# A convolution and selective-scan kernel: GpSimd multiplies two states at a time and takes over the sum of delta

## The reference

```python
xs = silu(conv5x5(x) + conv_b)                       # reshaped to (B, 96, 3136)
dts, Bs, Cs = split(einsum('kd,bdl->bkl', x_proj_w, xs))        # 6, 4, 4 rows
delta = softplus(einsum('dr,brl->bdl', dt_w, dts) + dt_b)
log_dA = maximum(delta[:, :, None, :] * A, LOG_EPS)  # A = -exp(A_logs), EPS = 1e-9
P = exp(cumsum(log_dA, axis=-1))
dB_u = delta[:, :, None, :] * Bs[:, None] * xs[:, :, None]
hs = P * cumsum(dB_u / maximum(P, EPS), axis=-1)
y = einsum('bdnl,bnl->bdl', hs, Cs) + xs * Ds
```

## Time and profile before

| | us |
|---|---|
| median of 3 runs | 4023.35 (4022.84 to 4023.77) |
| the profiled execution | 4020.36 |
| its span | 4018.6 |

### The profile page before, as it was taken

The page is one execution under the profiler, slowest core; times in us unless marked ns, Lnnn a source line. Parts: engine busy times, 40 slices in busy tenths (PEclk is TensorE's granted clock), DMA queues, the critical chain, the costliest instruction groups (busy, mean ns, idle before and its releaser), DMA issues. The chain is left out here.

```text
span 4018.6 us, 72697 instructions
## 1 busy us (share of the span) xinstructions
PE 3650.8 (91%) x22358; PEld 2646.6 (66%) x22358; DVE 3106.0 (77%) x4416; ACT 2571.1 (64%) x4292; POOL 2575.8 (64%) x2672
## 2 busy tenths in 40 slices
PE   6999999999999999997899998998989989899776
PEld 6888787979787887877565564664646646466322
DVE  3675758475756667570499998999989989989999
ACT  1463728172735546274688787787778878777754
POOL 0352717162634536270488888888979889888988
PEclk9999999999999999998799898998989989989877
DMA  7546473747465554428565564655546646465222
GB/s 225 170 138 204 104 250 95 251 102 234 109 200 149 164 181 125 149 76 181 130 177 143 162 170 124 172 152 147 164 127 181 169 125 173 129 168 158 86 75 60
DMA packets 383746, 612.84 MB, mean 153 GB/s; under 512 B 199967, under 2 KB 324152, under 8 KB 383048
## 3 DMA queue, kind: packets, MB, share of 16 engines
q1 hardware_dynamic: 383336, 607.74, 53.5%
HBM read 527.35 MB, written 80.28 MB: 151 GB/s over the span
## 5 line engine op out<-in xcount | busy, mean ns | idle before, releaser
L321 POOL TENSOR_TENSOR h_low<-act_h,h_high 128x448 fp32r<-128x448 f32 x448 | 598.0, 1354 | 724.1 <-ACT h_high L520 723.9
L515 ACT ACTIVATE act_h<-ps_up,b 128x448 f32<-128x448 f32 x672 | 408.7, 635 | 728.5 <-PE ps_up L633 728.2
L1348 PE MATMUL ps_y<-h,ident 128*128 128x448 f32 x1344 | 727.1, 629 | 144.3 <-POOL h L1036 113.1
L1036 POOL TENSOR_TENSOR h<-h,c_rows 128x448 f32<-128x448 f32 x672 | 763.7, 1136 | 51.2 <-DVE h L1126 5.7
L1023 POOL TENSOR_TENSOR u<-dxs,b_rows 128x448 f32<-128x448 f32 x672 | 764.5, 1138 | 27.9 <-DVE ps_q L1115 16.8
L1099 DVE TENSOR_TENSOR_SCAN ps_q<-d_a,q_last,ps_q 128x448 f32<-128x448 f32 x576 | 659.5, 1145 | 0.0
L1126 DVE TENSOR_TENSOR_SCAN h<-d_a,h_last,ps_q 128x448 f32<-128x448 f32 x576 | 645.3, 1120 | 0.0
L1300 PEld LDWEIGHTS ps_front<-win,taps 120*112 120x112 f32 x4608 | 540.5, 188 | 149.2 <-issue 147.2
L606 PE MATMUL ps_stage<-win,taps 124*112 124x112 f32 x6144 | 608.3, 261 | 2.7 <-DVE w_low L368 2.7
L606 PEld LDWEIGHTS ps_stage<-win,taps 124*112 124x112 f32 x6144 | 608.1, 178 | 3.2 <-DVE w_low L368 2.8
L1205 ACT ACTIVATE d_a<-delta,log_eps,a_neg 128x448 f32<-128x448 f32 x672 | 503.3, 750 | 114.0 <-DVE h L1126 58.5
(11 more groups left out here) (81 smaller groups left out, 6212.6 us busy)
## 6 DMA issues: line engine op xcount, KB each, us to landing
taps<-in_t_dram SPq DMA_DIRECT2D x192, 896.0 KB, 5.0
taps<-in_t_dram SPq DMA_DIRECT2D x192, 672.0 KB, 4.7
b_rows<-bc_dram SPq DMA_DIRECT2D x224, 224.0 KB, 3.0
c_rows<-bc_dram SPq DMA_DIRECT2D x224, 224.0 KB, 3.1
xres<-in_x_dram SPq DMA_DIRECT2D x224, 168.0 KB, 2.5
x_dram<-x1o SPq DMA_DIRECT2D x224, 168.0 KB, 2.0
x1pad<-x_dram SPq DMA_DIRECT2D x96, 392.0 KB, 6.0
out_dram<-y SPq DMA_DIRECT2D x168, 224.0 KB, 2.6
```

What stands on the lines that cost most here:

```text
L321: nc.gpsimd.tensor_tensor(h_low[u % 2][:, t, :], act_h[u % 2][:, t, :], h_high[u % 2][:, t, :], ALU.subtract).then_inc(h_low_ready[t], 1)
L515: nc.scalar.activation(act_h[u % 2][:, t, :], ps_up[t][:, 0:BT], ACT.Gelu, bias=b1[:, t:t + 1]).then_inc(gelu_done, 1)
L1036: nc.gpsimd.tensor_tensor(h[s % H_SLOTS][:, :], h[s % H_SLOTS][:, :], c_rows[n][:, :], ALU.mult).then_inc(hc_done, 1)
L1348: nc.tensor.matmul(total, ident[:, :], h[s % H_SLOTS][:, :], start=False, stop=(n == N - 1)).then_inc(y_added, 1)
```

## The change

It touches only layer 1.

- POOL works in pairs of states. `times_b` and `times_c` each handle two steps with one 128x2x448 instruction (dxs is read twice by a broadcast), and `h_last` keeps two columns at once. The buffers u, h and d_a become 2, 3 and 3 pairs (4, 6 and 6 tiles in place of 3, 6 and 7).
- ACT makes the Exp of the decays in pairs (`exp_a`, one 128x2x448 instruction every second step), still with one `clip_a` for each state. It works 4 steps ahead in place of 5.
- The sum that makes delta moves from DVE to POOL, which works from SBUF here: ACT first writes max(z, 0) from PSUM into delta with a Relu (line 1206 of the new kernel), and POOL adds the logarithm (line 1018 of the new kernel).
- SP issues the front's loads later: a load is placed where its slot is expected to be free, and behind the other DMAs of its step.

```diff
-ZSTEPS = 3
-U_SLOTS = 3
-U_AHEAD = U_SLOTS
-H_SLOTS = 6
+ZSTEPS = 4
+U_PAIRS = 2
+U_SLOTS = 2 * U_PAIRS
+H_PAIRS = 3
+H_SLOTS = 2 * H_PAIRS
-DA_SLOTS = 7
-DA_LEAD = 5
+DA_PAIRS = 3
+DA_SLOTS = 2 * DA_PAIRS
...
-        SUM_AT = (7, 9, 11)
-        DXS_AT, DXS_NOW = (8, 10), 1
+        SUM_AT, SUM_NOW = {3: 0, 4: 1}, {0: 2}
+        DXS_AT, DXS_NOW = {4: 0, 5: 1}, {1: 2}
...
+            def begin_at(load, k, unit):
+
+                last_use = {load_slab: turn_unit, load_taps: conv_unit}[load]
+                slots, pieces = {load_slab: (SLABS, 1), load_taps: (SLOTS2, HALVES)}[load]
+                free = unit_step[last_use[k - slots]] + pieces + 1 if k >= slots else 0
+                return max(unit_step[unit] - AHEAD, free)
...
-                    while todo and unit_step[todo[0][2]] <= s + AHEAD:
-                        load, k, _ = todo.pop(0)
-                        load(g + 1, False, k)
...
+                    while todo and begin_at(*todo[0]) <= s:
+                        load, k, _ = todo.pop(0)
+                        load(g + 1, False, k)
...
+            def sum_delta(f, b, t):
+                n = f * RUNS + b * TILES + t + 1
+                pool.wait_ge(z_step, n * ZSTEPS)
+                nc.gpsimd.tensor_tensor(delta[:, t, :], delta[:, t, :], z_log[t % Z_SLOTS][:, :],
+                                        ALU.add).then_inc(delta_ready, 1)
...
+                    pool.wait_ge(gated, g * S + 2 * p + 1 - U_SLOTS + 2)
+                nc.gpsimd.tensor_tensor(u[p % U_PAIRS][:, :, :], dxs[:, t, :].unsqueeze(1).broadcast_to([128, 2, BT]),
+                                        b_rows[:, n:n + 2, :], ALU.mult).then_inc(u_done, 2)
...
+                pool.wait_ge(h_done, g * S + 2 * p + 3)
...
+                nc.gpsimd.tensor_tensor(pair[:, :, :], pair[:, :, :], c_rows[:, n:n + 2, :],
+                                        ALU.mult).then_inc(hc_done, 2)
...
+                for p in range(S // 2):
+                    b, j = 2 * p // STEPS, 2 * p % STEPS // 2
...
+                    if p + 1 < S // 2:
+                        times_b(g, p + 1, p == 0 and first)
...
+                    if p > 0:
+                        times_c(g, p - 1)
+                    if prepare and j in SUM_AT:
+                        sum_delta(f, fb, SUM_AT[j])
...
-                    if (more or b + 1 < BANDS) and j in SUM_AT:
-                        sum_delta(f, fb, SUM_AT.index(j))
...
+                    act.wait_ge(clipped, (f * BANDS + b - 1) * STEPS + (t + 1) * N)
+                    act.wait_ge(dxs_ready, f * RUNS + (b - 1) * TILES + t + 1)
+                nc.scalar.activation(delta[:, t, :], z_bank(t)[:, 0:BT], ACT.Relu).then_inc(z_step, 1)
...
+                act.wait_ge(clipped, g * S + s + 2)
+                pair = d_a[s // 2 % DA_PAIRS]
+                nc.scalar.activation(pair[:, :, :], pair[:, :, :], ACT.Exp, bias=LOG_EPS).then_inc(d_a_ready, 2)
```

More of the change, by code:

```diff
@@ L948, in load_c @@
                     sp.wait_ge(hc_done, f * S + b * STEPS - N + n + 1)
[L949 removed]
+                sp.dma_start(c_rows[:, n, :], row(b, 1, n)).then_inc(c_in[n], 16)
             def first_slabs(f):
@@ L1061, in _ @@
+                    if j in SUM_NOW:
+                        sum_delta(g, b, SUM_NOW[j])
+                    if prepare and j in DXS_AT:
+                        times_x(f, fb, DXS_AT[j])
+                    if j in DXS_NOW:
+                        times_x(g, b, DXS_NOW[j], b == 0 and first)
+                times_c(g, S // 2 - 1)
             for t in range(TILES - 1):
+                sum_delta(0, 0, t)
                 times_x(0, 0, t, True)
-            for s in range(U_AHEAD):
-                times_b(0, s, True)
+            times_b(0, 0, True)
@@ L1140, in group @@
                     scan_h(g, s)
-            for t in range(TILES):
-                sum_delta(0, 0, t, True)
             if last:
@@ L1222, in group @@
                     f, fb = next_band(g, b)
-                    ahead = s + DA_LEAD
-                    if more or ahead < S:
+                    ahead = s + DA_SLOTS - 2
+                    pair_due = s % 2 == 0 and (more or ahead < S)
+                    if pair_due:
                         clip_a(g, ahead)
+                        clip_a(g, ahead + 1)
                     if more:
```

96 lines of the change are left out of this document (36 added, 60 removed).

## The result

The changed kernel is slower: 4071.86 us, median of 4 runs (4070.3 to 4078.44), against 4023.1 for the kernel before in the same comparison. The ratio is 1.0119, with a 95% interval of 1.01 to 1.0139. The prediction was 3941, with a range up to 4010. The profiled execution took 4078.44, its span is 4076.7.

What follows compares the result with a forecast made beforehand. DVE was taken as the bound, PE and POOL close behind. Its work of 1861 us plus 105 of waits gave 1966 against 2052.4; less 4 us of costs, a gain of 82, so 3941 us, range 3880 to 4010.

Steps and rivals of the forecast that it cites:

- DVE: the sums leave.: Moving 165 sums of 0.53 us off DVE, the pace setter, removes 87.5 us of its work; the largest term.
- POOL: does it stay under DVE?: POOL's band takes 32.8 us against DVE's new 33.6, at 2.05 per pair product, so POOL fits with 2% to spare.
- rivals 1 and 2: POOL sets the pace at 2.20 us a pair (3951, chance 0.10), or its 896-column products are slower still (0.09).
- the waits in front of the sum: POOL's waits for ACT's Ln, 1.2 us each, disappear in a 5.7 us slack before DVE stands; costed at nothing.
- PE.: PE gets h in pairs, up to 3.8 us later, against some 9 us of slack; its work is unchanged.
- This risk: PE, 93% busy, will be near 97% by the same records; taken as a risk and not as a bound.
- ACT.: ACT does 6 us more per group with less lead; DVE waits 6 us at a group's start, 3 in the burst.
- the prediction's own sign of being wrong: The forecast is wrong if DVE waits in bands 1 to 4 for u (POOL sets pace) or d_a (ACT does).
- Rival 3: ACT's short lead eats the gain: 12 us more per group, at its start and after the burst; 4025, chance 0.11.
- the halfway case of rival 2: POOL's pair product at 2.45 us, halfway from 2.20 to 2.71: a group is 262 us, the time 4119; rival's chance 0.09.
- Sum.: DVE work of 1861 us plus waits of 15 per group, 105 in all, the same as before by other causes: 1966.
- SP.: SP loads the C row ahead of the x1pad slab, ending DVE's 3.86 us wait behind it at a group's start.

Runs made afterwards that it cites:

- thin kernels: Kernels after and before, each without every second transpose of the first channel block in a group's front: 4027.2 us (0.9978) and 3996.33 us (0.9924).
- a_single7: Kernel after with the decays of the kernel before (7 single buffers, lead of 5 steps, one Exp per state): 4056.84 us, 1.0064.
- the square: Four kernels with POOL's pairs and single decays; u first or h with C first: sum on DVE 1.0047, 1.0082; sum on POOL 1.0051, 0.9938.
- b_lead4_sp_pool: Kernel before with six decay buffers, lead of four, new load order and POOL's pairs, u first: 4045.83 us, 1.0047.

## Why the prediction was wrong

**DVE: the sums leave.** The work is right: the page's busy time of DVE fell by 84.1 us (3106.0 to 3021.9), forecast 87.5. The size on the path was wrong. As the change orders POOL it gained nothing with single decays (1.0047 to 1.0051) and cost 39 us with pairs of Exps (1.0023 to 1.0119); with h ahead of u it gained 58.

**POOL: does it stay under DVE?** The durations and the spacing were right, and the band of 32.8 against 33.6 about so (POOL is busy 32.4 us in the mean of bands 1 to 5), and rivals 1 and 2 fall: a pair starts 2.04 us behind the other (2586.10 to 2588.14), and DVE doesn't wait for u. The Trainium skill, "Perfetto Trace Analysis", section "GPSIMD Engine Instruction", has a GpSimd instruction timed by the spacing of starts and not by its span; the trace agrees, in that the record of this product says 2.08 and the next starts after 2.04. What failed is the step behind it: the waits in front of the sum and the lag of up to 5.7 us behind them, of which it says "I cost them at nothing in the bands 1 to 4". I asked only who waits for u. POOL makes two things, and h with C, which the change puts behind u and the sums, has a consumer that is just as near its limit. A lag that did not reach the gate in the kernel after still reached PE, as h with C 9.1 us after the first state's h in place of 3.3. The swap, which changes only which of the two goes first, is worth 66 us of the 131 by which the forecast was off.

**PE.** "It gets h in pairs, up to 3.8 us later" against a slack of 9. It is some 7.5 us later in band 2 (9.2 against 1.7), and the slack was measured at the wrong place. Long before h's buffer is missed, PE's front pieces, which stand behind the y sum in its queue, are late for ACT's evictions. This risk was named and given no price. POOL's pairs alone cost 29 us with the lead of 5 (0.9975 to 1.0047), and 51 to 74 us, in either order, with the lead of 4 (0.9897 or 0.9919 against 1.0047 or 1.0082). This can be the rest of the error, but it was measured in other kernels, and the prices need not add to the swap's 66.

**ACT.** Where the waits come to light was right (d_a at the group's start and after bursts, u no longer, C rows far less), and the sequence at the start too. So did the prediction's own sign of being wrong come true: DVE waits for d_a in bands 1 and 3. The cause was not right. The short lead alone makes the kernel before faster, and an Exp ahead of the evictions gains nothing. Rival 3 (4025) is 47 us from the measured time by the wrong mechanism, and the halfway case of rival 2 (4119), which did not happen either, is as near: that closeness is luck. ACT's work grew by 1.9 us a group (206.3 to 208.2), forecast 6. The bursts of bands 3 and 6, which the prediction left out, cost their share as well.

**Sum.** The waits per group, 15 forecast, are 35: 14.8 in band 0 (6 forecast), 7.5 in the burst of band 5 (3), 1.6 at the loop's return (2), and 10.8 in bands 1, 3 and 6 (2 elsewhere and 2 for the lack of reserve). The claim that the waits stay "the same as before, by other causes" is where the 248 - 105 = 143 us lie. Each new wait was priced with all other engines on time.

**SP.** Right in direction; worth 0.25% by itself and 1.7% in the changed kernel.

**What stays open.** The path from PE's late y sum to each late eviction was read at the places shown and not followed for every wait. The swap shows that h's lateness costs, and the thin kernels that PE's work lies on the chain; that PE's queue order carries it is argued from the trace. A longer lag of PE's y sums, which would test it, wasn't tried. Neither the lag nor PE's wait for h ranks the kernels by itself: `a_single7` has the longest lag (11.3 us over all bands) and is faster than the kernel after, and PE waits longer for h with the sum on VectorE (89.7 and 92.6 us in the two kernels of the square) than in the kernel after (71.1). How much of band 0 is the low clock's own doing is open as well. How the price of the pairs divides between PE's wait for h and other waits (POOL stood 44.2 us for xd in `b_lead4_sp_pool`, 7.6 in the kernel before) is not known either.

## What to carry to other kernels

When an engine gets more work and keeps under the pace setter, list each of its products with its consumer, and order them by who has least slack: a lag that is free for one can be dear for the other, and a swap of two lines was worth 66 us here, where the move of 88 us of work gained 58 in the better order and lost up to 39 in the worse. In a closed chain of four engines that are busy 79 to 92% of the time, the engine that waits tells only where the chain closes; measure the lag of each hand-over as well, before and after. Work in pairs adds the second item's wait to the first, so look for slack of a whole step at the next engine in line. And where one stretch is long in some groups and short in others of the same loop, compare the granted clock in both before blaming the code.
